# A vision block on one core: the dense stage freed from VectorE, and the last token tile's top-k moved into the rounds

## What is computed

```python
q = (hidden_states @ w_queries.T).reshape(b, t, 2, h, n)
sim = jnp.einsum('btphn,hkpn->pbthk', q, keys)
sx, ix = jax.lax.top_k(sim[0], k)
sy, iy = jax.lax.top_k(sim[1], k)
all_scores = (sx[..., :, None] + sy[..., None, :]).reshape(b, t, h, k * k)
all_idx = (ix[..., :, None] * nk + iy[..., None, :]).reshape(b, t, h, k * k)
scores, pos = jax.lax.top_k(all_scores, k)
indices = jnp.take_along_axis(all_idx, pos, axis=-1)
de = down_embed[indices]
ue = up_embed[indices]
ew = jnp.einsum('btd,bthkd->bthk', hidden_states, de)
ew = jax.nn.silu(ew) * jax.nn.softmax(scores, axis=-1)
experts_states = jnp.einsum('bthk,bthkd->btd', ew, ue)
mlp = jax.nn.silu(hidden_states @ w_gate.T) * (hidden_states @ w_up.T) @ w_down.T
return mlp + experts_states
```

## Time and profile before

| | us |
|---|---|
| median of 3 runs | 273.3 (273.24 to 273.79) |
| the profiled execution, in all | 275.31 |
| its span, first to last instruction | 273.5 |
| TensorE busy | 247.0 (90%) |
| VectorE busy | 180.7 (66%) |
| ScalarE busy | 57.0 (21%) |
| GpSimd busy | 54.7 (20%) |
| mean granted clock | 0.975 |

### The profile page before, as it was taken

One profiled execution on the slowest core, in us unless ns is written; L12 is line 12 of the kernel. 1 busy time (PEld: TensorE's weight loads), 2 busy tenths in 40 slices (PEclk: granted clock), 3 DMA queues, 4 the chain that ended last, 5 costly groups with the idle time before them and its releaser, 6 DMA issues.

```text
span 273.5 us, 4832 instructions
## 1 busy us (share of the span) xinstructions
PE 247.0 (90%) x1956; PEld 203.7 (74%) x1956; DVE 180.7 (66%) x455; ACT 57.0 (21%) x104; POOL 54.7 (20%) x71
## 2 busy tenths in 40 slices
PE   3998985889768899899999999899979999999996
PEld 2575653668543488889898899888968888888773
DVE  0037199678885449999999999799968767511100
ACT  1101127343444242323132743100000000000000
POOL 5013146114422523225052620000000000000000
PEclk9999999999975799999999999999999999999999
DMA  7960000130002271061125430300000000000000
GB/s 253 386 233 0 2 0 0 55 104 29 25 20 74 63 218 54 7 205 60 40 54 178 127 105 1 91 0 2 0 19 2 0 19 2 0 19 2 19 0 12
DMA packets 14805, 16.99 MB, mean 62 GB/s; under 512 B 848, under 2 KB 12992, under 8 KB 14784
## 3 DMA queue, kind: packets, MB, share of 16 engines
q1 hardware_dynamic: 13776, 15.70, 17.9%
q10 hardware_dynamic: 1008, 1.00, 1.1%
HBM read 15.48 MB, written 1.21 MB: 61 GB/s over the span
## 4 chain that ended last, share of the span: by engine, by line
PE 58%; DVE 34%; issue 3%; ACT 3%; DMA 1%; DVEq 0%; POOL 0%; ACTq 0%
PE ps L1067 23%; PE ps L1030 9%; PE ps L820 7%; PE ps L1089 5%; DVE topi L696 3%; DVE big L795 3%; DVE top L693 3%; PE ps L971 3%; PE ps L1064 3%; DVE big L547 2%; PE ps L897 2%; DVE xn L515 2%; PE ps L938 2%; PE ps L847 2%; DVE red L589 1%
## 5 line engine op out<-in xcount | busy, mean ns | idle before, releaser
L1067 PE MATMUL ps<-ue,big 128*128 128x256 f32 (+1 forms) x320 | 72.3, 381 | 1.4 <-DVE big L795 1.4
L1067 PEld LDWEIGHTS ps<-ue,big 128*128 128x128 f32 (+1 forms) x320 | 57.2, 182 | 12.1 <-DVE big L795 1.8
L1030 PE MATMUL ps<-hn_hi,de_hi 128*128 128x296 f32 x128 | 40.7, 318 | 2.1 <-ACT big L482 1.1
L795 DVE TENSOR_TENSOR big<-ps,big 128x1024 f32<-128x1024 f32 (+1 forms) x19 | 22.7, 1197 | 26.9 <-PE ps L1089 26.2
L1030 PE MATMUL ps<-hn_lo,de_hi 128*128 128x296 f32 x128 | 38.4, 300 | 0.0
L1030 PE MATMUL ps<-hn_hi,de_lo 128*128 128x296 f32 x128 | 38.2, 299 | 0.0
L482 ACT ACTIVATE big<-ps 128x592 f32<-128x592 f32 x32 | 21.1, 665 | 44.5 <-PE ps L1030 44.4
L1030 PEld LDWEIGHTS ps<-hn_hi,de_hi 128*128 128x128 f32 x128 | 24.1, 188 | 4.7 <-DVE actT L742 1.9
L1030 PEld LDWEIGHTS ps<-hn_lo,de_hi 128*128 128x128 f32 x128 | 24.1, 188 | 1.2 <-issue 1.2
L1030 PEld LDWEIGHTS ps<-hn_hi,de_lo 128*128 128x128 f32 x128 | 24.1, 188 | 0.0
L820 PE MATMUL ps<-big 128*111 128x256 f32 (+1 forms) x72 | 19.3, 426 | 4.7 <-DMA big<-in_w_tok 4.7
(11 more groups left out here) (113 smaller groups left out, 337.9 us busy)
## 6 DMA issues: line engine op xcount, KB each, us to landing
de<-in_down_t SPq DMA_DIRECT2D x16, 256.0 KB, 2.8
ue<-in_up_e SPq DMA_DIRECT2D x4, 1024.0 KB, 5.9
big<-in_patches SPq DMA_DIRECT2D x6, 296.0 KB, 5.2
big<-in_w_tok ACTq DMA_DIRECT2D x6, 128.0 KB, 5.9
big<-in_w_qkv SPq DMA_DIRECT2D x1, 768.0 KB, 8.6
h_scratch<-big SPq DMA_DIRECT2D x5, 111.0 KB
late<-in_keys_bd SPq DMA_DIRECT2D x1, 512.0 KB, 9.7
downT<-in_wdown_t SPq DMA_DIRECT2D x1, 512.0 KB, 9.3
```

The costliest lines, as they stand in the source:

```text
L795: chain(nc.vector.tensor_tensor(dst, pv, dst, ALU.mult), g_ready)
L1030: last = mm(ps[:, 2 + 2 * (e % 2) + a, 0:HALF], half[:, (e // 2) % SPLITS, k, own], src[:, k, a * HALF:(a + 1) * HALF], start=(n == 0), st ...
L1067: last = mm(acc, sil[:, e, j * 128:j * 128 + Q * v], ue[:, e, :], start=False, stop=(e == EX - 1))
```

## The change

On TensorE the up product moves to banks 0 and 1, and from expert 16 on the experts use three bank pairs in turn (2, 4, 0). So no expert before number 18 waits for the gated product; the next up product does. The gate has two buffers in SBUF. The keys are stored for two heads at a time, and the similarities of a tile are four matmuls of 256 columns, each over 64 rows; one signal stands for both sides. ScalarE's exponential is taken for tiles 0 to 3 before the silu of expert 18, and for tile 4 after the last silu. On VectorE the logits of tiles 0 to 3 are one instruction; after the best keys of tile 4 it computes the weights of tiles 0 to 3 and the first four slots, and only then the best sums of tile 4. The places of tile 4 follow in round 6 of the rounds, its weights in round 9. SyncE loads the residual, which now lies over the second gate buffer, after the last gated product.

```diff
+GATED = 16
+EXP_AT = 18
...
-        sg = slots[:, 6 * D:6 * D + T]
+        sg = (slots[:, 6 * D:6 * D + T], rows[:, 0:T])
...
+        def dense_bank(e):
+
+            return 2 + 2 * (e % 2) if e < GATED else (2, 4, 0)[(e - GATED) % 3]
...
             sp.wait_ge(st_h, 16 * NG)
             sp.wait_ge(pe_s, EX)
+            sp.wait_ge(gu_done, IC)
...
-                    if j == TILES - 1 and i == 5:
-
-                        act.wait_ge(lg_ready, TILES)
-                        nc.scalar.activation(ex[:, :, :, :], ex[:, :, :, :], ACT.Exp).then_inc(lg_exp, 1)
+                    if e == EXP_AT:
+
+                        act.wait_ge(lg_ready, 1)
+                        nc.scalar.activation(ex[:, 0:IC], ex[:, 0:IC], ACT.Exp).then_inc(lg_exp, 1)
...
-                    if j >= 1:
-                        act.wait_ge(gu_done, j)
+                    if j >= 2:
+                        act.wait_ge(gu_done, j - 1)
...
+            act.wait_ge(lg_ready, 2)
+            nc.scalar.activation(ex[:, IC:TILES], ex[:, IC:TILES], ACT.Exp).then_inc(lg_exp, 1)
...
+            for j in range(IC):
+                best_keys(j, 0)
+                best_keys(j, 1)
+                best_pairs(j)
+                if j == IC - 1:
+                    logits(0, IC)
+                places(j)
+                gated_product(j)
+            best_keys(IC, 0)
+            best_keys(IC, 1)
+            weights(0, IC, 1)
             for i in range(RING):
                 build_slots(i)
+            best_pairs(IC)
+            logits(IC, TILES)
...
+                if i == 6:
+                    places(IC)
+                elif i == 9:
+                    weights(IC, TILES, 2)
...
-            def sims(j, p):
+            def sims(j):
                 if j >= 1:
-                    pe.wait_ge(sim_read, 2 * (j - 1) + p + 1)
-                mm(ps[:, 6 + p, :], qT[:, p, j * 128:(j + 1) * 128],
-                   keysBD[:, p, :, :].rearrange("p h k -> p (h k)"), start=True, stop=True).then_inc(pe_sim, 1)
+                    pe.wait_ge(sim_read, 2 * j)
+                for p in range(2):
+                    for i in range(2):
+                        own = slice(2 * FN * i, 2 * FN * (i + 1))
+                        last = mm(ps[:, 6 + i, p * 2 * NK:(p + 1) * 2 * NK],
+                                  qT[own, p, j * 128:(j + 1) * 128], keys2[own, p, :], start=True, stop=True)
+                last.then_inc(pe_sim, 1)
...
-                    if j >= 1 and i < 2:
-
-                        pe.wait_ge((gate_act, gu_done)[i], j)
+                    if j >= 1 and i == 0:
+
+                        pe.wait_ge(gate_act, j)
+                    if e == GATED + 2:
+
+                        pe.wait_ge(gu_done, IC)
                     if e % 2 == 0:
                         pe.wait_ge(split_ready, 2 * (e // 2 + 1))
                     if e >= 2:
-                        pe.wait_ge(sil_ready, e - 1)
+                        pe.wait_ge(sil_ready, e - 1 if e < GATED + 3 else e - 2)
...
-                    pe.wait_ge(sil_ready, e)
-                    gated(4, (up_hi, up_lo), j, pe_gu)
+                    if j >= 1:
+                        pe.wait_ge(gu_done, j)
+                    gated(0, (up_hi, up_lo), j, pe_gu)
```

More of the change, by code:

```diff
@@ L685, in build_slots, with best_keys, best_pairs @@
                     .broadcast_to([128, c, 2 * Q, EX, 2]), ALU.mult), slots_ready)
[L687 to L697, removed]
+            def best_keys(j, p):
+                dve.wait_ge(pe_sim, j + 1)
+                simv = ps[:, 6:8, p * 2 * NK:(p + 1) * 2 * NK].rearrange("p a (h k) -> p a h k", h=2)
+                behind()
+                for hh in range(FH):
+                    chain(nc.vector.max(top[:, p, hh, :], simv[:, hh // 2, hh % 2]))
+                behind()
+                for hh in range(FH):
+                    chain(nc.vector.max_index(topi[:, p, hh, :], top[:, p, hh, :], simv[:, hh // 2, hh % 2]),
+                          sim_read if hh == FH - 1 else dve_chain)
+            def best_pairs(j):
                 behind()
@@ L705, in _, with places @@
                 for hh in range(FH):
[L706 removed]
+                    chain(nc.vector.max(best[:, j, hh, :], cf[:, hh, :]))
                 behind()
                 for hh in range(FH):
[L709 to L712 removed]
+                    chain(nc.vector.max_index(besti[:, hh, :], best[:, j, hh, :], cf[:, hh, :]))
+            def places(j):
                 behind()
@@ L737, in _ @@
                                               over[:, :, :], ALU.max))
[L739 to L756, removed]
@@ L766, in _, with gated_product @@
-            for j in range(TILES):
-                for a in range(2):
-                    chain(nc.vector.tensor_tensor(wsel[:, j, :, a], own,
-                                                  by_pairs(packT[:, j, 2 + a, :]).unsqueeze(2)
-                                                  .broadcast_to([128, TT // 2, Q, 2]), ALU.mult))
+            def gated_product(j):
+                dve.wait_ge(gate_act, j + 1)
+                dve.wait_ge(pe_gu, j + 1)
+                chain(nc.vector.scalar_tensor_tensor(halves(actT[:, j, :]), halves(sg[j % 2]), WSCALE,
+                                                     ps[:, 0:2, 0:HALF], ALU.mult, ALU.mult), gu_done)
@@ L1029, in _ @@
                         for n, (half, src, k) in enumerate(parts):
-                            last = mm(ps[:, 2 + 2 * (e % 2) + a, 0:HALF], half[:, (e // 2) % SPLITS, k, own],
+                            last = mm(ps[:, dense_bank(e) + a, 0:HALF], half[:, (e // 2) % SPLITS, k, own],
                                       src[:, k, a * HALF:(a + 1) * HALF], start=(n == 0), stop=(n == len(parts) - 1))
@@ L1033, in _ @@
                     if e == 1:
[L1034 to L1035 removed]
+                        sims(0)
                     e += 1
```

69 lines of the change are left out of this document (45 added, 24 removed).

## The result

The changed kernel takes 276.62 us (median of 6 runs, 275.95 to 278.27), the kernel before 273.31 (273.24 to 274.91, 6 runs beside them). The ratio is 1.0112, 95% interval 1.0077 to 1.0146: slower, by 3.1 us by the ratio and 3.3 by the medians. Forecast were 275.8 and a range of 272.3 to 277.7. Executions of one kernel fall into groups some 1.5 us apart (29 of the kernel before lie near 273.5 or near 275), so that a median over few of them can move by that much.

The account below looks back on a forecast made before the run. No engine was taken as the limit all the way; handovers between TensorE and VectorE bound the kernel. From 273.3 us, dense stage -3.6, rounds +3.75 and clock +2.35 gave 275.8 us, range 272.3 to 277.7.

Parts of the forecast that it names:

- The dense stage: Stage before the rounds: VectorE's fourth gated product starts expert 18, 14 experts follow; gains 3.6 us, bounds 2.4 to 4.7.
- Tile 0: First token tile of the dense stage: GpSimd's split lies over VectorE's cast to topf and costs about 1.0 us.
- The rounds: Tile 4's places delay the product of round 7, TensorE's wait grows from 1.41 to 5.2 us; loses 3.75 us.
- The clock: After the 5.2 us wait TensorE runs at half speed for some 4.7 us; costs 2.35 us, between 1.5 and 3.5.
- The first rival: TensorE's clock holds after the long wait in the rounds, so no measurable change: 273.4 us; chance 20%.
- The second rival: VectorE has slack in rounds 4 to 7, so the places are free and the time is 269.7 us; chance 7%.
- The third: Dense stage's similarity matmuls gain nothing from row groups: dense term 2.4 us, time 277.0 us; chance 5%.

Follow-up runs that it names:

- run with the old banks: Changed kernel with tile 4's places behind product 7, but up product in banks 4 and 5 and two bank pairs: 276.98 us, ratio 1.0087 to the kernel before.
- places ahead of the rounds: Changed kernel with tile 4's places moved from round 6 to behind the logits of tile 4: 275.23 us, ratio 1.0043 to the kernel before.
- run with the filled wait: Changed kernel with 11 extra matmuls nobody reads ahead of TensorE's wait for the product of round 7: 274.11 us, ratio 1.0007 to the kernel before.
- run with the gated product first: Changed kernel, tile 4's places and the slots of rounds 10, 14, 18 one round later, tile 3's gated product ahead of its places: 266.72 us, ratio 0.9750.

## Why the prediction was right

**The dense stage: -3.6 forecast, -3.72 measured.** The form was right: VectorE's fourth gated product starts expert 18, and 14 experts later round 0 begins (144.30 to 167.36, 23.06 us, which is 14 x 1.64 + 0.1). Two counts inside it were off. VectorE's product came 0.2 us earlier behind the stage's start than forecast, since it lost 1.8 us to GpSimd and not the 2.05 I took. The wait before expert 18 was 1.53 instead of 2.3 us mostly because TensorE got there some 0.5 later, as a similarity step costs 1.26 and not 1.15; that was free, since TensorE waits there anyway. Tile 0 was met as forecast. Timeline of after, the split and the cast:

```profile
102.51 1.29 POOL L368 TENSOR_TENSOR de_lo<-de,de_hi 128x512 fp32r<-128x512 f32 x1
102.59 1.26 DVE L711 CAST topf<-topi 128x64 f32<-128x64 uint32 x1
...
142.96 0.61 DVE L748 TENSOR_TENSOR pack<-pick,over 128x32 f16<-128x32 f32 x1
```

The cast starts 0.08 behind the split and takes 1.26 instead of 0.20; it ends 0.05 behind the split's end. The Trainium skill (SBUF — State Buffer, "SBUF: two separate sides") says that of the two engines the one that starts first keeps the shared ports for its whole instruction; the trace agrees in both directions, here VectorE pays, in the earlier trace rows at 104.42 GpSimd did. Tiles 1 to 3 cost 0.1 each at the cast and 0.42 once at 142.96. The run with the old banks shows how much hangs on phase: there VectorE loses 4.0 us in the same tiles, against 1.8.

**The rounds: +3.75 forecast, +4.15 measured.** The product of round 7 comes 3.80 later behind that of round 6, as counted. The other 0.35 nobody forecast: a wait of 0.46 us before the second of four slots in round 3. Timeline of after, VectorE:

```profile
176.48 0.29 DVE L683 TENSOR_TENSOR eqx<-iota_rep,packT 128x256 f16<-128x256 f16 x1 [0.46 <-DVE late L690]
```

It waits for VectorE's own earlier instruction by the profile. The four slots take the same 0.35 us longer in all runs but the one with the places ahead of the rounds, which is as quick there as the kernel before. What causes it stays open.

**The clock: +2.35 forecast, +2.30 measured.** The step rested on one fall in the attention. The run with the filled wait shows that it was the right cause: same restart, clock up, 2.13 us less. The other 0.17 is a term that the prediction put at nothing, tile 4's weights in round 9: with them there and the clock up the last stage takes 71.05 and 71.06 (wait filled, places ahead), with them in round 11 at most 70.88. In the filled run the product of round 11 starts 18.32 us behind the restart, in the kernel before 17.94. The first rival (the clock holds, 20%) is that very run, at 1.0007, where its sum was 273.4.

**The second rival** (the shadow is real, 7%) is settled by two runs: the places cost nearly the same ahead of the rounds (31.33 us to the restart against 31.73), and nothing one round later. **The third** (row groups don't overlap, 5%) falls with 1.26 us per similarity step against 1.71; the attention's scores had given 1.15.

**One number was wrong without harm.** VectorE was to wait some 4 us before the first round's product and waits 1.51. I had costed the weights of four tiles and the first four slots as if nothing met them; in the profile GpSimd's splits take some 3.0 us from VectorE in the weights and slots between 149 and 158, 0.97 of it in this row of after's timeline, which is 1.23 elsewhere:

```profile
155.93 2.20 DVE L690 TENSOR_TENSOR late<-eqx,wsel 128x2048 f16<-128x2048 f16 x1
```

The slack was eaten there and not in the sum. It mattered for what to do next: with only 1.5 us free ahead of round 0 the places couldn't have gone there either, as the run showed.

**What the prediction didn't say**, though its rows held it: that VectorE's list from the first MAX8 to the product of round 7 takes 100.55 us before with one gap of 1.21, and that behind this gap VectorE waits for nobody. So reordering inside the list can win about what the gap holds, as the run with the gated product first does (1.4 us); the rest has to be taken past that product.

## What to carry to other kernels

Before moving a step "into the shadow", find the next point at which somebody waits for that engine: inside the stretch that ends there every place is as dear as another, but for idle time that a step can fill, and just behind it the same step can be free. A wait that grows costs twice on TensorE, once as time and once through the clock behind it; matmuls that nobody reads can hold the clock, but it is better to remove the wait. Where two engines hand over to each other in turn, a gain on one of them counts only together with the step on the other.

## What the runs showed of the hardware

- TensorE's clock behind a pause, as the rows have it: after 0.82 us (wait filled), 1.24, 1.41, 1.53 and 1.76 the granted clock stayed at 1.00; after 2.43 (old banks), 3.26 (places ahead) and 5.57 (after) it went to 0.50, the 1.2 GHz level, and came back 3.4 to 4.4 us behind the restart. The Trainium skill (TensorE: Matmul & The Clock Gate, "HAM oscillation — how this bites in real kernels") describes such falls for kernels that wait for DMA in each pass of a loop; here a single wait in the middle of dense work was enough. The length of one pause does not decide it everywhere: in the attention of after the clock fell behind pauses of 0.44 and 0.43 us, with TensorE busy for 64 to 89% of each microsecond from 70 to 74, where in the kernel before it stayed up behind the same two. TensorE's timeline of after, then windows of 1 us for TensorE alone (duration, busy time and records, granted clock, DMA):

```profile
73.22 1.60 PE L980 MATMUL ps<-big 128*111 128x256 f32 x4 [0.43 <-ACT big L458]
```

```profile
73.00:74.00 1.00, 0.78 (x3) 0.86 0.16 53
74.00:75.00 1.00, 1.00 (x5) 0.50 0.00 0
```

- Four matmuls of 64 rows by 256 columns in two row groups took 1.06 us from start to the next matmul, and 0.1 more in the matmul ahead and in that one, where two of 128 rows by 512 columns take 1.31 to the next start and 0.40 more in that one: 1.26 against 1.71.
- A short VectorE instruction can become six times as long when a GpSimd instruction starts just ahead of it (0.20 to 1.26 us), and a shift of some tenths of a us between the engines decides it.
